# A graph network with a soft mixture of experts: the output product on 32-row strips

## The chip, the cores and the metric

The kernel runs on one core of a Trainium2 chip. The metric is the device time of one execution in microseconds (us); lower is better. The core has TensorE (PE in the profile; its weight loads are PEld), VectorE (DVE), ScalarE (ACT), GpSimd (POOL) and SyncE (SP), and 16 DMA engines.

## The reference

6250 nodes with 768 numbers each, 106250 edges sorted by destination. Two graph convolutions over the layer-normed input, added to it; then a soft mixture of experts with 8 experts of 4 slots each, 32 slots in all, added again:

```python
x = x + gnn(layernorm(x), edges, W1, b1, W2, b2)          # two GCN layers
# ffn on layernorm(x), m = 6250 tokens, n = 8 experts, p = 4 slots
logits  = einsum('bmd,dnp->bmnp', Xn, sp)
D = softmax(logits, axis=1)                                # over the tokens
C = softmax(logits over n*p, axis=2)                       # over the 32 slots of a token
X_tilde = einsum('bmd,bmnp->bnpd', Xn, D)                  # [32 slots, 768]
H = gelu(einsum('bnpd,ndh->bnph', X_tilde, W_down) + b_down)
Y_tilde = einsum('bnph,nhd->bnpd', H, W_up) + b_up         # [32 slots, 768]
Y = einsum('bnpd,bmnp->bmd', Y_tilde, C)                   # the output product
x = x + Y
```

## The kernel before

Nodes lie in T = 49 tiles of 128 (the last has 106). Each engine has its own program; semaphores order them. All arithmetic is in f32 but for the one-hot products of the start.

**Start.** SP loads the edges' destinations; VectorE makes one-hot matrices of them in 25 groups (L897 and L899, both operands in SBUF), and TensorE counts with them (L1274). GpSimd clears and fills the constants one after the other: iotas, memsets, two selects on `own_expert` and two on `in_quarter` (the loops at L604 and L608), then selects that make `ident`, `below` and `steps_down` (L615 to L620), each of which counts up `ready_consts`. TensorE begins behind all three. Behind `steps_down` GpSimd's queue issues the first weight loads (L627). TensorE turns each weight, and ScalarE moves it away (L698) between groups of statistics over x (L713, L724); it then scales x and stores it as the first layer's table. `in_quarter` is a [128, 4] table of masks: column c is 1 on the rows 32c to 32c + 31 and 0 elsewhere.

**Layers.** Both layers gather neighbours' rows with indirect DMAs (L659), sum them on VectorE (L1113) and multiply by the weights on TensorE.

**Experts.** TensorE mixes all tokens into the 32 slots (L1430), applies the down weights (L1447), and, after the gelu, the up weights (L1455, and the bias with 8 rows at L1457). The left operand holds each slot four times, so that `acc` gets Y_tilde four times, one copy on each strip of 32 rows.

**Output product.** The coefficients `cw` of four tiles at a time (a group; there are 13, the last holds tile 48 alone) are turned by one transpose (`turn_c`, L1465) into `work`, and ScalarE copies them to one of two `cT` buffers (L872): rows 32c to 32c + 31 of it belong to tile 4g + c. To take the right rows, VectorE makes four masked copies of `acc` (L1248, into hid, the two self_row buffers and agg; tile t uses copy t mod 4, `y_quarters`), each zero outside of its own strip. Tile t's product then contracts all 128 rows of `cT` with copy t mod 4, in two halves of 384 columns; each half shows up as two records, so a tile has four (L1479). It writes to one of three pairs of PSUM banks in turn (acc, fixed, left), and starts only when the add of tile t - 3 has read its pair. VectorE adds the tile to x in an output buffer (L1255). ScalarE's queue issues the store (L865), and tile t's store waits until that of tile t - 4 has landed. The copy of the next group's cT stands in the same queue ahead of a group's stores. The last 16 tiles of x do not fit and are loaded again by SP (L500): five before this stage, eleven in it, each behind an early tile's store.

Of the kernel before, what the change touches and what calls it, by code (L numbers as in the profile page):

```python
# [11 lines left out]
P = 128  # L12
# [4 lines left out]
H = D // 2  # L17
# [14 lines left out]
EXPERTS, SLOTS_PER, HID = 8, 4, D // 8  # L32
SLOTS = EXPERTS * SLOTS_PER
# [23 lines left out]
def build(nc, a):  # L57
# [6 lines left out]
    ALU = mybir.AluOpType  # L64
# [3 lines left out]
    with ctx:  # L68
        def sb(name, shape, dt=f32):
            return ctx.enter_context(nc.sbuf_tensor(name, shape, dt))  # L70
# [4 lines left out]
        def sem(name):  # L75
            return ctx.enter_context(nc.semaphore(name))
# [49 lines left out]
        self_row = sb("self_row", [P, 2, D])  # L126
        agg = sb("agg", [P, D])
# [3 lines left out]
        hid = sb("hid", [P, D])  # L131
# [3 lines left out]
        bup = sb("bup", [EXPERTS, D])  # L135
        sel = sb("sel", [EXPERTS, 4, SLOTS])
        own_expert = sb("own_expert", [SLOTS, EXPERTS])
        in_quarter = sb("in_quarter", [P, 4])
        hidT = sb("hidT", [HID, SLOTS])
        hid_blocks = sb("hid_blocks", [HID, EXPERTS * BLOCK])  # L140
        cT = sb("cT", [P, 2, P])
# [4 lines left out]
        acc = ps("acc", [P, 2, 512])  # L146
# [7 lines left out]
        def halves(ap):  # L154
            return ap.rearrange("p (h n) -> p h n", h=2)
# [55 lines left out]
        def layer_sems(l):  # L211
# [10 lines left out]
        F = {n: sem("F_" + n) for n in (  # L222
            "turned", "w_in", "w_staged", "mixed_done", "out_ready", "c_turned", "c_moved", "y_done", "blocks_clear",
            "exp_in", "exp_done", "root_in", "root_done", "gelu_in", "gelu_done", "top_ready", "sumd_ready", "sumd_done",
            "c_ready", "mix_ready", "mixT_ready", "down_done", "down_picked", "up_done", "y_slots_ready")}
# [153 lines left out]
        def full(i, k, t):  # L379
# [24 lines left out]
        accs = [acc, fixed, left]  # L404
        hid_lhs = hid_blocks[:, 0:EXPERTS * P].rearrange("p (n c) -> p n c", n=EXPERTS)
        hid_own = hid_blocks[:, :].rearrange("p (n c) -> p n c", c=BLOCK)[:, :, 0:P].rearrange(
            "p n (c q) -> p n c q", c=4)[:, :, :, 0:SLOTS_PER]
        y_quarters = [hid[:, :], self_row[:, 0, :], self_row[:, 1, :], agg[:, :]]
        ffn = flat[:, 4 * D + T * SLOTS:]
        wdown = WT[0][:, :, :].rearrange("p k (n h) -> p k n h", n=EXPERTS)  # L410
        wup = ffn[0:HID, 0:EXPERTS * D].rearrange("p (n d) -> p n d", n=EXPERTS)
# [178 lines left out]
        def _(pool):  # L590
# [7 lines left out]
                pool.memset(ap, v).then_inc(s["cleared"], 1)  # L598
            pool.memset(hid_blocks[:, :], 0.0).then_inc(F["blocks_clear"], 1)
            pool.memset(own_expert[:, :], 1.0).then_inc(F["blocks_clear"], 1)  # L600
            pool.memset(in_quarter[:, :], 1.0).then_inc(F["blocks_clear"], 1)
            pool.wait_ge(F["blocks_clear"], 3)
            for ap, width, cols in ((own_expert[:, :], SLOTS_PER, EXPERTS), (in_quarter[:, :], SLOTS, 4)):
                pool.affine_select(out=ap, in_=ap, compare_op=ALU.is_ge, fill=0.0, base=0, pattern=[[-width, cols]],  # L604
                                   channel_multiplier=1).then_inc(F["blocks_clear"], 1)
            pool.wait_ge(F["blocks_clear"], 5)
            for ap, width, cols in ((own_expert[:, :], SLOTS_PER, EXPERTS), (in_quarter[:, :], SLOTS, 4)):
                pool.affine_select(out=ap, in_=ap, compare_op=ALU.is_gt, fill=0.0, base=width, pattern=[[width, cols]],  # L608
                                   channel_multiplier=-1).then_inc(F["blocks_clear"], 1)
            pool.iota(zero_row[:, :], pattern=[[1, 1]], base=ZERO_ROW, channel_multiplier=1,  # L610
                      allow_small_or_imprecise_dtypes=True).then_inc(s["iotas"], 1)
            pool.iota(slot_of[:, :], pattern=[[P, PICKS]], base=0, channel_multiplier=1,
# [3 lines left out]
                               base=0, pattern=[[-1, P]], channel_multiplier=1).then_inc(s["ready_consts"], 1)  # L616
            pool.affine_select(out=below[:, :], in_=ones[:, :], compare_op=ALU.is_gt, fill=0.0,
                               base=0, pattern=[[1, P]], channel_multiplier=-1).then_inc(s["ready_consts"], 1)
            pool.wait_ge(s["ready_consts"], 1)
            pool.affine_select(out=steps_down[:, :], in_=ident[:, :], compare_op=ALU.not_equal, fill=-1.0,  # L620
                               base=-1, pattern=[[-1, P]], channel_multiplier=1).then_inc(s["ready_consts"], 1)
# [63 lines left out]
        def _(act):  # L685
# [54 lines left out]
            for n in range(RELOADED, len(loads)):  # L740
                t = loads[n]
# [111 lines left out]
                    act.wait_ge(F["exp_in"], len(THIRDS) + 1)  # L853
                    act.activation(cw[:, :, :], cw[:, :, :], ACT.Exp).then_inc(F["exp_done"], 1)
            act.wait_ge(F["gelu_in"], 1)
            act.wait_ge(F["blocks_clear"], 7)
            act.activation(hid_own, hidT[:, :].rearrange("p (n q) -> p n q", n=EXPERTS).unsqueeze(2)
                           .to_broadcast([HID, EXPERTS, 4, SLOTS_PER]), ACT.Gelu).then_inc(F["gelu_done"], 1)

# [22 lines left out]
        def _(dve):  # L882
# [345 lines left out]
                                     ident[0:EXPERTS, 0:EXPERTS].unsqueeze(1).unsqueeze(3)  # L1228
                                     .to_broadcast([EXPERTS, 4, EXPERTS, SLOTS_PER])))
            dve.wait_ge(F["down_done"], 1)  # L1230
            dve.wait_ge(F["blocks_clear"], 7)
            spread = hid[0:SLOTS, :].rearrange("p (n h) -> p n h", n=EXPERTS)
            for h in range(2):
                ns = slice(h * EXPERTS // 2, (h + 1) * EXPERTS // 2)
# [9 lines left out]
                                       bdT.unsqueeze(2).to_broadcast([HID, EXPERTS, SLOTS_PER]), ALU.add))  # L1244
            dve.sem_inc(F["gelu_in"], 1)
            dve.wait_ge(F["up_done"], 1)
            for c, y in enumerate(y_quarters):
                dve.tensor_scalar(halves(y), acc[:, :, 0:H], in_quarter[:, c:c + 1], None, ALU.mult  # L1248
                                  ).then_inc(F["y_slots_ready"], 1)
            for t in range(T):  # L1250
                dve.wait_ge(F["y_done"], t + 1)
                if t >= KEPT:
# [6 lines left out]
        def _(pe):  # L1259
# [205 lines left out]
                pe.transpose(tp[0:cols, g % 2, 0:P], cw[:, 4 * g:4 * g + cols // SLOTS, :].rearrange("p t q -> p (t q)"),  # L1465
                             ident[:, :]).then_inc(F["c_turned"], 1)
            turn_c(0)
            pe.wait_ge(F["y_slots_ready"], 4)
            for g in range(QUADS):
                if g + 1 < QUADS:  # L1470
                    turn_c(g + 1)
                pe.wait_ge(F["c_moved"], g + 1)
                ts = range(4 * g, min(4 * g + 4, T))
                for t in ts:
                    if t >= 3:
                        pe.wait_ge(F["out_ready"], t - 2)
                    k = SLOTS * len(ts)
                    for h in range(2):
                        m = pe.matmul(accs[t % 3][:, h, 0:H], cT[0:k, g % 2, :], y_quarters[t % 4][0:k, h * H:(h + 1) * H],  # L1479
                                      start=True, stop=True)  # L1480
                    m.then_inc(F["y_done"], 1)

# [22 lines left out]
```

## Time and profile before

| | us |
|---|---|
| median of 3 runs | 3048.95 (3045.4 to 3049.35) |
| span of the profiled execution, first to last instruction | 2757.7 |
| TensorE busy | 2105.0 (76%) |
| VectorE busy | 1809.1 (66%) |
| GpSimd busy | 1840.6 (67%) |
| ScalarE busy | 535.4 (19%) |

The profiled execution is given by its span alone; the time that it took in all stands nowhere in the page. The median of the runs is 291.25 us above the span, which holds what lies ahead of the first instruction and behind the last. The mean granted TensorE clock is 0.934 of full speed.

### The profile page before, as it was taken

How to read it: one execution, taken by the hardware profiler on the slowest of the kernel's cores; microseconds unless marked ns; L12 is line 12 of the kernel's file. 1: busy time of each engine (PE TensorE's matmuls, PEld its weight loads, DVE VectorE, ACT ScalarE, POOL GpSimd, SP SyncE). 2: the span in 40 equal slices, each digit the busy share in tenths (PEclk: the TensorE clock that was granted, in tenths of full speed). 3: DMA queues.
4: the chain of work that ended last, by engine and by line, in shares of the span. 5: the costliest groups of instructions: out<-in, count | busy, mean ns of one | idle time of the engine just before them, and what ended most of it. 6: DMA issues, size and time to landing. Idle time of an engine off the chain costs nothing.

```text
span 2757.7 us, 27634 instructions
## 1 busy us (share of the span) xinstructions
PE 2105.0 (76%) x7712; PEld 1248.5 (45%) x7713; DVE 1809.1 (66%) x2350; ACT 535.4 (19%) x985; POOL 1840.6 (67%) x1853
## 2 busy tenths in 40 slices
PE   6716777777787777787768877787787787888888
PEld 6703444444444444444434544444444454545334
DVE  7755666666676667666556766676766666666226
ACT  7950111111111111111101212211121222221310
POOL 3157777777777777777567777777777777776000
PEclk9999999999989989989978999999999999899899
DMA  9498999999999999999779999999999999998738
GB/s 331 155 411 304 315 321 322 322 321 322 322 325 327 327 329 326 325 317 319 269 278 328 373 341 339 338 339 342 344 346 344 342 342 343 336 338 306 252 111 322
DMA packets 237825, 876.71 MB, mean 318 GB/s; under 512 B 63260, under 2 KB 64044, under 8 KB 237756
## 3 DMA queue, kind: packets, MB, share of 16 engines
q0 software_dynamic: 143808, 671.74, 69.2%
q1 hardware_dynamic: 66132, 162.17, 16.0%
q10 hardware_dynamic: 27836, 42.21, 4.2%
q8 instruction: 23, 0.38, 0.1%
q14 instruction: 26, 0.21, 0.0%
HBM read 826.10 MB, written 82.00 MB: 329 GB/s over the span
## 4 chain that ended last, share of the span: by engine, by line
DMA 31%; POOL 26%; issue 16%; PE 12%; DVE 9%; ACT 4%; POOLq 0%; DVEq 0%; ACTq 0%
DMA rows<-table_layer,gidx 28%; POOL rows L659 26%; DVE acc L1113 6%; PE work L1355 3%; PE left L1381 3%; PE left L1430 2%; DMA table_layer<-xstage 2%; DVE agg L1113 1%; ACT logits L724 1%; ACT xsT L713 1%; DVE agg L1158 1%; DMA out_x<-xstage 1%; PE acc L1479 1%; ACT acc L783 1%; PE work L1367 1%
## 5 line engine op out<-in xcount | busy, mean ns | idle before, releaser
L659 POOL DMA_INDIRECT rows<-table_layer,gidx x1764 | 1761.6, 999 | 537.9 <-issue 449.4
L1113 DVE TENSOR_TENSOR acc<-acc,rows 128x768 f32<-128x768 f32 x1176 | 1134.7, 965 | 705.7 <-DMA rows<-table_layer,gidx 651.6
L1381 PE MATMUL left<-rows,hot 128*128 128x384 f32 x1960 | 847.9, 561 | 455.5 <-DMA rows<-table_layer,gidx 448.3
L1355 PE MATMUL work<-WT,aggT 128*128 128x384 f32 x2352 | 798.7, 497 | 43.9 <-DVE row_idx L1022 42.5
L1381 PEld LDWEIGHTS left<-rows,hot 128*128 128x128 f32 x1960 | 369.4, 209 | 792.8 <-DMA rows<-table_layer,gidx 625.7
L1355 PEld LDWEIGHTS work<-WT,aggT 128*128 128x128 f32 x2352 | 453.8, 195 | 386.8 <-DVE row_idx L1022 76.0
L783 ACT ACTIVATE acc<-rows 128x768 f32<-128x768 f32 x98 | 79.8, 814 | 667.1 <-DVE agg L1158 582.2
L813 ACT ACTIVATE aggT<-fixed 128x768 f32<-128x768 f32 x98 | 79.4, 810 | 514.1 <-PE fixed L1331 514.1
L800 ACT ACTIVATE xsT<-fixed 128x768 f32<-128x768 f32 x49 | 39.7, 810 | 459.1 <-PE fixed L1342 459.1
L793 ACT ACTIVATE ynext<-hid,dinv 128x768 f32<-128x768 f32 x49 | 45.8, 934 | 339.0 <-DVE hid L1128 339.0
L1158 DVE TENSOR_TENSOR agg<-left,agg 128x768 f32<-128x768 f32 x98 | 93.9, 958 | 8.7
L1113 DVE TENSOR_TENSOR agg<-acc,self_row 128x768 f32<-128x768 f32 x98 | 93.8, 958 | 4.4
L1274 PE MATMUL left<-rows 125*128 125x49 bf16 x850 | 79.2, 269 | 19.8 <-POOL steps_down L620 19.8
L1331 PEld LDWEIGHTS fixed<-ident,agg 128*128 128x128 f32 x588 | 71.8, 143 | 38.4 <-issue 17.6
L1331 PE MATMUL fixed<-ident,agg 128*128 128x128 f32 x588 | 82.3, 277 | 6.8 <-DVE agg L1158 6.8
L1274 PEld LDWEIGHTS left<-rows 125*128 125x128 bf16 x850 | 78.4, 142 | 20.1 <-POOL steps_down L620 19.5
L1367 PEld LDWEIGHTS work<-sp_c,xsT 128*128 128x128 f32 x588 | 75.5, 197 | 16.2 <-ACT xsT L800 3.0
L1072 DVE TENSOR_TENSOR hot<-acc,left_node 128x640 f32<-128x640 f32 x98 | 79.9, 815 | 0.4 <-DVE xsT L1049 0.4
L634 POOL DMA_INDIRECT rows<-src_windows,ynext x49 | 51.4, 1049 | 42.6 <-DVEq L937 28.0
L1367 PE MATMUL work<-sp_c,xsT 128*128 128x32 f32 x588 | 72.4, 275 | 3.2 <-ACT xsT L800 2.5
L1297 PEld LDWEIGHTS work<-xsT,before_end 128*128 128x128 f32 x490 | 65.9, 201 | 16.0 <-DVE before_end L994 2.4
L897 DVE TENSOR_TENSOR rows<-rows 125x4352 bf16<-125x4352 bf16 x25 | 60.6, 2424 | 17.6 <-PE left L1274 17.6
(307 smaller groups left out, 1253.2 us busy)
## 6 DMA issues: line engine op xcount, KB each, us to landing
self_row<-table_layer SPq DMA_DIRECT2D x98, 384.0 KB, 6.6
rows<-table_layer,gidx POOLq DMA_INDIRECT x1764, 5.7
xstage<-in_x SPq DMA_DIRECT2D x67, 384.0 KB, 8.1
xs<-in_x SPq DMA_DIRECT2D x58, 384.0 KB, 7.5
xnew<-xs SPq DMA_DIRECT2D x49, 384.0 KB, 5.0
table_layer<-ynext SPq DMA_DIRECT2D x48, 384.0 KB, 5.1
table_layer<-xstage ACTq DMA_DIRECT2D x40, 384.0 KB, 11.6
xstage<-xnew SPq DMA_DIRECT2D x21, 384.0 KB, 5.8
```

What stands on the lines that cost most here:

```text
L659: pool.indirect_dma_start(rows[:, slot, :], None, table[l][0:ROWS, :], bass.IndirectOffsetOnAxis(ap=gidx[:, k % 2, slot:slot + 1], axis=0) ...
L783: act.activation(acc[:, :, 0:H], halves(rows[:, SLOT["own", 0], :]), ACT.Copy).then_inc(S["first_copied"], 1)
L813: act.activation(halves(aggT[:, :, :].rearrange("p k n -> p (k n)")), turned[:, :, 0:H], ACT.Copy).then_inc(S["aggT_ready"], 1)
L1072: dve.tensor_tensor(hot[:, b, 0:LEFT, :], iota_ps.unsqueeze(1).to_broadcast([P, LEFT, P]), left_node[:, ds(t, 1), 0:LEFT].rearrange("p t c ...
L1113: dve.tensor_tensor(acc[:, :, 0:H] if n < OWN - 1 else halves(agg[:, :]), acc[:, :, 0:H], halves(row), ALU.add).then_inc(S["added"], 1)
L1158: dve.tensor_tensor(halves(agg[:, :]), left[:, :, 0:H], halves(agg[:, :]), ALU.add).then_inc(S["agg_ready"], 1)
L1274: m = pe.matmul(mm[:, 0, 0:T], oh_low[:, g % 2, :, j], oh_high[:, g % 2, :, j], start=(g == 0 and j == 0), stop=(g == GROUPS - 1 and j == ...
L1297: m = pe.matmul(found[:, c // 3, c % 3, :], before_end[:, c * P:(c + 1) * P], cands[:, ds(t, 1), :], start=True, stop=True)
L1331: m = pe.transpose(turned[:, kc // 3, (kc % 3) * P:(kc % 3 + 1) * P], agg[:, kc * P:(kc + 1) * P], ident[:, :])
L1355: m = pe.matmul(work[:, h, 0:H], aggT[:, kc, :], WT[l][:, kc, h * H:(h + 1) * H], start=kc == 0, stop=kc == KC - 1)
L1367: m = pe.matmul(work[:, 1, H:H + SLOTS], xsT[:, 0, kc, :], sp_c[:, kc, :], start=kc == 0, stop=kc == KC - 1)
L1381: m = pe.matmul(left[:, h, 0:H], hot[:, b, c, :], rows[:, slot, h * H:(h + 1) * H], start=c == 0, stop=c == LEFT - 1)
```

## The change

The masks, their memset and their two selects go; the semaphore `blocks_clear` ends at 4 instead of 7. One plain copy of `acc` into hid takes the place of the four masked ones. Tile t's product contracts only the 32 rows of its own strip, on both operands. The number of matmuls and their columns stay.

```diff
-        in_quarter = sb("in_quarter", [P, 4])
...
-        y_quarters = [hid[:, :], self_row[:, 0, :], self_row[:, 1, :], agg[:, :]]
+        y_copies = hid[:, :]
...
-            pool.memset(in_quarter[:, :], 1.0).then_inc(F["blocks_clear"], 1)
+            pool.wait_ge(F["blocks_clear"], 2)
+            pool.affine_select(out=own_expert[:, :], in_=own_expert[:, :], compare_op=ALU.is_ge, fill=0.0, base=0,
+                               pattern=[[-SLOTS_PER, EXPERTS]], channel_multiplier=1).then_inc(F["blocks_clear"], 1)
             pool.wait_ge(F["blocks_clear"], 3)
-            for ap, width, cols in ((own_expert[:, :], SLOTS_PER, EXPERTS), (in_quarter[:, :], SLOTS, 4)):
-                pool.affine_select(out=ap, in_=ap, compare_op=ALU.is_ge, fill=0.0, base=0, pattern=[[-width, cols]],
-                                   channel_multiplier=1).then_inc(F["blocks_clear"], 1)
-            pool.wait_ge(F["blocks_clear"], 5)
-            for ap, width, cols in ((own_expert[:, :], SLOTS_PER, EXPERTS), (in_quarter[:, :], SLOTS, 4)):
-                pool.affine_select(out=ap, in_=ap, compare_op=ALU.is_gt, fill=0.0, base=width, pattern=[[width, cols]],
-                                   channel_multiplier=-1).then_inc(F["blocks_clear"], 1)
+            pool.affine_select(out=own_expert[:, :], in_=own_expert[:, :], compare_op=ALU.is_gt, fill=0.0, base=SLOTS_PER,
+                               pattern=[[SLOTS_PER, EXPERTS]], channel_multiplier=-1).then_inc(F["blocks_clear"], 1)
...
             dve.wait_ge(F["up_done"], 1)
-            for c, y in enumerate(y_quarters):
-                dve.tensor_scalar(halves(y), acc[:, :, 0:H], in_quarter[:, c:c + 1], None, ALU.mult
-                                  ).then_inc(F["y_slots_ready"], 1)
+            dve.tensor_copy(halves(y_copies), acc[:, :, 0:H]).then_inc(F["y_slots_ready"], 1)
...
-            pe.wait_ge(F["y_slots_ready"], 4)
+            pe.wait_ge(F["y_slots_ready"], 1)
...
-                    k = SLOTS * len(ts)
+                    strip = slice(SLOTS * (t % 4), SLOTS * (t % 4 + 1))
                     for h in range(2):
-                        m = pe.matmul(accs[t % 3][:, h, 0:H], cT[0:k, g % 2, :], y_quarters[t % 4][0:k, h * H:(h + 1) * H],
+                        m = pe.matmul(accs[t % 3][:, h, 0:H], cT[strip, g % 2, :], y_copies[strip, h * H:(h + 1) * H],
                                       start=True, stop=True)
```

## Rows read from the trace of the kernel before

**Rows 1.** The page, chain that ended last, by line, share of the span

```profile
DMA rows<-table_layer,gidx 28%; POOL rows L659 26%; DVE acc L1113 6%; PE work L1355 3%; PE left L1381 3%; PE left L1430 2%; DMA table_layer<-xstage 2%; DVE agg L1113 1%; ACT logits L724 1%; ACT xsT L713 1%; DVE agg L1158 1%; DMA out_x<-xstage 1%; PE acc L1479 1%; ACT acc L783 1%; PE work L1367 1%
```

**Rows 2.** Windows over the output stage: length, busy us, PEclk, DMA share, GB/s

```profile
2688.00:2707.80 19.80, 19.13 (x62) 10.98 (x61) 14.48 (x16) 0.82 (x3) 0.00 (x0) 1.00 1.02 402
...
2714.30:2724.00 9.70, 9.63 (x31) 5.74 (x32) 5.93 (x7) 0.57 (x3) 0.00 (x0) 1.00 1.03 412
2724.00:2748.60 24.60, 23.64 (x76) 13.36 (x74) 17.98 (x19) 1.10 (x4) 0.00 (x0) 1.00 0.77 303
2748.70:2757.70 9.00, 0.00 (x0) 0.00 (x0) 0.00 (x0) 0.00 (x0) 0.00 (x0) 0.59 0.14 50
```

**Rows 3.** The chain in order of time: start us, us, what

```profile
2673.51 1.50 PE acc L1457 x4
...
2679.36 2.56 PE acc L1479 x4
...
2740.89 0.11 PE work L1465
...
2744.87 1.29 PE left L1479 x4
2746.16 1.50 PE acc L1479 x4
```

**Rows 4.** Timeline: start us, us, engine, line; idle before in brackets

```profile
2673.44 0.94 PEld L1457 LDWEIGHTS acc<-bup,sel 8*128 8x128 f32 x4 [0.55 <-issue]
...
2675.04 1.02 DVE L1248 TENSOR_SCALAR hid<-acc,in_quarter 128x768 f32<-128x768 f32 x1 [14.25 <-PE acc L1457]
...
2677.82 1.01 DVE L1248 TENSOR_SCALAR agg<-acc,in_quarter 128x768 f32<-128x768 f32 x1
...
2746.09 0.94 PEld L1479 LDWEIGHTS acc<-hid,cT 32*128 32x128 f32 x4 [0.55 <-issue]
```

**Rows 5.** Windows around the copies, columns as in rows 2

```profile
2675.30:2678.80 3.50, 0.00 (x0) 0.00 (x0) 3.50 (x4) 0.27 (x1) 0.00 (x0) 0.98 0.00 0
2678.80:2681.80 3.00, 2.92 (x6) 1.71 (x7) 0.03 (x1) 0.28 (x1) 0.00 (x0) 0.50 0.00 0
```

**Rows 6.** Timeline of the start

```profile
14.46 1.02 DVE L899 TENSOR_TENSOR rows<-rows 125x1666 bf16<-125x1666 bf16 x1
14.55 0.98 POOL L604 TENSOR_SCALAR_AFFINE_SELECT in_quarter<-in_quarter 128x4 f32<-128x4 f32 x1
...
15.39 2.42 DVE L897 TENSOR_TENSOR rows<-rows 125x4352 bf16<-125x4352 bf16 x1
15.60 2.26 POOL L608 TENSOR_SCALAR_AFFINE_SELECT own_expert<-own_expert 32x8 f32<-32x8 f32 x1
...
17.73 1.02 DVE L899 TENSOR_TENSOR rows<-rows 125x1666 bf16<-125x1666 bf16 x1
...
17.82 0.97 POOL L608 TENSOR_SCALAR_AFFINE_SELECT in_quarter<-in_quarter 128x4 f32<-128x4 f32 x1
...
18.96 0.28 POOL L615 TENSOR_SCALAR_AFFINE_SELECT ident<-ident 128x128 f32<-128x128 f32 x1
...
19.45 0.28 POOL L620 TENSOR_SCALAR_AFFINE_SELECT steps_down<-ident 128x128 f32<-128x128 f32 x1
...
27.81 0.82 ACT L698 ACTIVATE WT<-work 128x768 f32<-128x768 f32 x1 [3.38 <-PE work L1267]
```

**Rows 7.** Timeline: the plain copies from PSUM on VectorE

```profile
156.98 0.55 DVE L1049 COPY xsT<-left 128x377 f32<-128x377 f32 x1 [1.84 <-PE left L1305]
...
2647.46 0.36 DVE L1223 COPY aggT<-work 128x192 f32<-128x192 f32 x1 [0.73 <-PE work L1442]
```

**Rows 8.** Groups by line from 2660 us on: xcount, busy us, mean ns, idle before

```profile
L1255 DVE TENSOR_TENSOR xstage<-acc,xstage 128x768 f32<-128x768 f32 x7 | 6.7, 958 | 2.6 <-PE acc L1479 2.6
```

**Rows 9.** Windows over the mix of all tokens (L1430), columns as in rows 2

```profile
2600.00:2620.00 20.00, 20.00 (x63) 6.82 (x62) 0.27 (x1) 6.36 (x17) 0.00 (x0) 1.00 0.48 116
```

**Rows 10.** Waits of TensorE in the output stage: us in total, times, longest

```profile
PE acc L1479 <- ACT cT L872: 1.0, 1, 1.0
```

More of the change, by code:

```diff
@@ L855, in _ @@
             act.wait_ge(F["gelu_in"], 1)
-            act.wait_ge(F["blocks_clear"], 7)
+            act.wait_ge(F["blocks_clear"], 4)
             act.activation(hid_own, hidT[:, :].rearrange("p (n q) -> p n q", n=EXPERTS).unsqueeze(2)
@@ L1230, in _ @@
             dve.wait_ge(F["down_done"], 1)
-            dve.wait_ge(F["blocks_clear"], 7)
+            dve.wait_ge(F["blocks_clear"], 4)
             spread = hid[0:SLOTS, :].rearrange("p (n h) -> p n h", n=EXPERTS)
```

## The prediction

> **What bounds the kernel now.** I read the page first, for where the edited stages lie in the chain of waits. Gathers and their issue on GpSimd hold 28% and 26% of it, in layers that the diff does not touch; the output product, PE acc at L1479, shows up with 1% [rows 1]. So three short places count: the start of the program, the copies ahead of the output product, and the output stage, together under 100 of 2757.7 us.
>
> The output stage comes next, cut into stretches [rows 2]. From 2688 to 2724 the DMA engines are full, 402 to 412 GB/s: stores of finished tiles and reloads of the last sixteen share them. From 2724 to 2748.6 they move 303 GB/s and TensorE is busy 23.6 of 24.6 us. The last 9 us are the last store (50 GB/s), and they follow the last add whatever the stage before did. So the stage is bound by transfers first and by TensorE later. The chain in order of time gives the pace of the second part: 1.29 us for a tile's four matmul records, 0.11 us for the transpose between groups of four, 1.50 us for the last tile [rows 3]. A group of four tiles is 4 x 1.29 + 0.11 = 5.27 us.
>
> The timeline ahead of it shows the four masked copies one after the other, while TensorE does nothing [rows 4], and the windows give the granted clock: 0.98 in that gap, 0.50 just after it (the 1.2 GHz level) [rows 5], 1.00 again later [rows 2]. The last view is the first 28 us, where the removed GpSimd work sits [rows 6].
>
> **The start of the program.** Three GpSimd instructions go: a memset and two selects on in_quarter, 0.98 and 0.97 us by their durations [rows 6]. TensorE cannot start before steps_down, and GpSimd's first weight load is issued right behind it; ScalarE then waits 3.38 us for that weight's transposes and is busy from there without a gap. An earlier load therefore moves everything behind it. Adding up the rows gives about 2.0 us. But the rows say more: selects on 128x4 and 32x8 take 0.98, 2.26 and 0.97 us, while those on 128x128 take 0.28 each. The three slow ones end at 15.53, 17.86 and 18.79 us (start plus duration), each 0.04 or 0.05 us behind the end of a VectorE one-hot operation (15.48, 17.81, 18.75); the fast ones run once VectorE is idle. I take it that a select gets through once per VectorE operation. Then without in_quarter the select on ident comes through at 17.86, below at 18.79, and steps_down ends at about 19.05 instead of 19.73: 0.7 us gained, not 2.0. I take 0.7 and keep 2.0 for the range.
>
> That reading has a rule behind it. The Trainium skill ("SBUF — State Buffer", on the shared port pair) says that a GpSimd operation which reads SBUF and a VectorE operation with two SBUF inputs lock each other out for a whole instruction; the ends in these rows agree. By the rule the saving is 0.7 us, by the durations alone 2.0.
>
> **The copies.** Before, from the first copy's start to the end of tile 0 by the chain takes 2681.92 - 2675.04 = 6.88 us: 3.80 of copies, 0.52 with the transpose, 2.56 for four matmul records at half clock [rows 3, 4]. After, there is one plain copy. No row shows a plain copy of 128x768 from PSUM; two smaller ones take 0.36 us at 192 columns and 0.55 at 377 [rows 7], a slope that gives 0.95, and the masked one takes 1.02. I take 0.99. TensorE's gap, which by the chain begins at 2675.01, then ends at about 2676.07 instead of 2678.84. Since the clock was still 0.98 in the gap and fell only at its end, I count full clock afterwards: 0.25 for the transpose and 1.50 for the tile, the price of the only 32-row tile that the trace has. That is 0.99 + 0.04 + 0.25 + 1.50 = 2.78, a gain of 4.10 us. If the clock fell all the same, 1.4 of this is lost; that bound is kept. The stage that follows is bound by transfers, and since those start earlier by the same time and carry the same bytes, the 4.10 us pass through it.
>
> **The output products.** Each tile has four records before and after, with 384 columns; only the rows shrink, from 128 to 32. Fewer rows alone buy nothing: the last tile with 32 rows and the bias product with 8 (L1457) take no less than a full one. What changes is the neighbours. Two costs or gains come in.
>
> First, a switch between full-height and 32-row products. Both 8-row (L1457) and 32-row (last tile) groups take 1.50 us instead of 1.29, and in both the weight load is not pulled ahead but starts behind 0.55 us of idle [rows 3, 4]. So 0.21 us per entry; I give the same to the way back, which no row prices apart (at least nothing, at most the 0.55 us of that idle). Before, this is paid at the very end; after, each group holds one full-height transpose between strips, so 2 x 0.21 = 0.42 us per group.
>
> Second, neighbouring tiles now sit in different 32-row strips of the array and write to different PSUM tiles (acc, fixed, left). No row here has two products in different strips, so the price is bounded: at worst nothing overlaps (1.29 per tile), at best VectorE's add becomes the limit, 0.96 us per tile [rows 8], about 4.2 us per group with handovers. In between lies what an in-order engine could do: records of one tile share a strip and stay serial, so only the last record of a tile can run beside the first of the next, and four tiles take 16 - 3 = 13 slots of 0.3225 us, 4.19 us. I take this middle value because the switch cost shows that TensorE treats 32-row products as a mode of their own.
>
> The Trainium skill ("TensorE: Matmul & The Clock Gate", Part 3) states that matmuls in different row groups run concurrently while a single one with 32 rows costs as much as with 128; its "TensorEngine Tiling (Array Packing)" adds that changing the mode drains the engine. The second speaks against the change and agrees with the 0.21 us here; the first no row shows.
>
> Sum per group: 4.19 + 0.11 + 0.42 = 4.72, against 5.27: 0.55 us less. It counts only where TensorE is the limit, behind the stretch in which transfers rule. The last tile starts at 2746.16; counted back at 5.27 us, six full groups (tiles 24 to 47) fit from about 2714.5 on, which is where that stretch gives way: 6 x 0.55 = 3.3 us. In the groups before, extra or saved time hides behind the full DMA queue. The last tile no longer has a switch ahead of it and can overlap tile 47: 1.50 becomes 0.97, 0.5 us. Against this, the DMA engines are full until 2724, and ScalarE's queue holds each cT copy behind the stores of the group before, which wait for earlier stores to land. A faster TensorE meets that wait once more; I set 0.5 us for it, half of the 1.0 us that it idles for ahead of tile 24 now [rows 10].
>
> **The sum.** -0.7 - 4.1 - 3.3 - 0.5 + 0.5 = -8.1 us. Made against the profiled execution, whose span is 2757.7: 2749.6 after. Its time outside the span is not given; the median of the runs, 3048.95, lies 291.25 above the span, and nothing in the change touches that part. So 3048.95 - 8.1 = 3040.9 us. The runs shown spread from 3045.4 to 3049.35; about 0.2%, 6 us, is what a measurement tells from no change.
>
> **Rivals.**
> **No overlap between strips.** Switches cost and nothing is given back: 6 x 0.42 = 2.5 lost, 0.2 won at the last tile, so -0.7 - 4.1 + 2.3 = -2.5: 3046.5 us. For it: no overlapping products in the trace, and TensorE's f32 products go as two records each, of which I do not know whether they keep the array to themselves. Against it: only that 32-row groups are visibly handled apart. The result would be within 0.2%.
> **Free switches.** If the drain seen at the last tile hides behind other strips' work, a group is bound by the add: 4.2 + 0.1 us, six groups give 5.8 instead of 3.3, and 3038.4 us.
> **The clock falls in the output stage.** With a quarter of the rows in use, the granted clock might drop to the 1.2 GHz level for whole stretches. A tile then costs 2.56 us [rows 3]; at 13 slots of 0.64 a group takes about 8.7 us, twelve groups and a tile 107 us from 2676.3 to 2783, against 2747.7: some 35 us more, 3084 us. It decides from about eleven slow tiles in the second part on (11 x 1.27 = 14 us eat the 8.1 and 6 more). Against it: the stage before the experts keeps TensorE at 1.00 with products of only 32 columns of weights [rows 9], and the 8-row and 32-row groups ran at full pace, though for 1.5 us only.
> **The rest of the program answers.** The gathers hold the largest share of the chain, and their arrivals can shift with an earlier start: I allow the 4 us by which the runs shown differ, either way.
>
> **How the numbers follow.** Overlap as forecast, with the free-switch case as its upper end: 0.62. No overlap: 0.30. Clock: 0.04. Anything else: 0.04. The likeliest case reaches from 3036 to 3044; the range takes in no overlap with its spread, and below, free switches with the 2.0 us start (3037.1) and the spread of the runs: 3034 to 3048. Within the overlap case three of four chances lie beyond 0.2% faster, in the others hardly one in ten: faster 0.50, within 0.2% 0.44, slower 0.06.
>
> **What the profile after would show.** The first steps_down at about 19.05 us, ident's select lengthened to about 2 us; one VectorE copy of 1.0 us ahead of the product; granted clock 1.00 right behind it; tile 0 done 4 us earlier within the stage; starts of records of neighbouring tiles closer than 0.32 us at the edges between tiles, 4.7 us per group behind tile 24; 303 GB/s raised to about 335. A pace of 5.7 us per group shows the first rival, granted clock near 0.5 the third. I am wrong above all if strips do not overlap, or if the earlier transfers do not come through the full-queue stretch.

## The result, and the profile after

The median of nine runs after is 3064.82 us (3056.27 to 3071.34), beside 3048.95 (3038.65 to 3053.65) for nine runs of before: ratio 1.0053, 95% interval 1.0041 to 1.0064. The change costs 0.5%, 15.9 us; 8.1 us of gain were forecast.

Chips differ: on those of the experiments before takes 2759.0 to 2759.4 us instead of 3049, and the ratio is the same (1.0052). The profiled execution of before (span 2757.7) is of that faster kind. So spans are compared below within one kind of chip, or by stretches of the output stage, which hold no gathers.

The page of after, busy time by engine: TensorE has 111 us more than before (2105.0), in as many matmuls.

```profile
PE 2216.2 (72%) x7712; PEld 1319.0 (43%) x7713; DVE 1808.2 (59%) x2347; ACT 533.5 (17%) x985; POOL 1838.7 (60%) x1850
```

Not all of it is the change's: 91 us are products of the layers (L1349), which take 540 ns each on this chip, with 238.0 us of idle ahead of them in all, and 497 ns in the profile of before, with 43.9. On the other kind of chip the two kernels have 2113.2 and 2131.9 us, 18.7 apart. Where these are, the windows of the output stage show; after, columns as in rows 2 (length, busy us, PEclk, DMA share, GB/s):

```profile
2969.00:2971.00 2.00, 1.91 (x6) 0.80 (x5) 0.31 (x1) 0.06 (x1) 0.00 (x0) 1.00 0.00 0
2971.00:2975.00 4.00, 3.30 (x13) 1.42 (x13) 0.64 (x1) 0.50 (x2) 0.00 (x0) 0.51 0.00 0
...
2980.00:2990.00 10.00, 9.66 (x29) 4.32 (x25) 4.11 (x5) 0.55 (x2) 0.00 (x0) 0.50 0.98 334
2990.00:3000.00 10.00, 9.33 (x22) 4.25 (x21) 5.86 (x7) 0.28 (x1) 0.00 (x0) 0.50 1.03 377
...
3040.00:3050.00 10.00, 9.33 (x24) 4.06 (x21) 6.25 (x7) 0.28 (x1) 0.00 (x0) 0.50 0.49 190
```

The granted clock falls to 0.50 (1.2 GHz) as before [rows 5], but it never comes back: 0.50 to the end, where before had 1.00 [rows 2]. A closer window shows that it fell during the copy, ahead of the first strip, which starts at 2972.11:

```profile
2971.20:2972.10 0.90, 0.40 (x1) 0.18 (x1) 0.44 (x1) 0.02 (x1) 0.00 (x0) 0.50 0.00 0
```

So what has to be explained is not the fall, which before has too, but that the clock stays down. The DMA engines, full at first, end at half of their share. The timeline shows the strips at work (start us, us, engine, line; idle before in brackets):

```profile
2970.69 0.96 DVE L1243 COPY hid<-acc 128x768 f32<-128x768 f32 x1 [14.25 <-PE acc L1451]
...
2971.70 0.48 PE L1459 MATMUL work<-ident,rows 128*128 128x128 f32 x1 [0.79 <-DVE hid L1243]
...
2972.11 1.00 PE L1473 MATMUL acc<-hid,cT 32*128 32x384 f32 x1
...
2972.12 1.00 PE L1473 MATMUL fixed<-hid,cT 32*128 32x384 f32 x1
...
2972.13 1.00 PE L1473 MATMUL left<-hid,cT 32*128 32x384 f32 x1
```

Three tiles start 0.01 us apart and run beside each other in full, not at their edges only. In the later groups two start together and the third some 0.7 us behind, when its pair of banks comes free. The chain in order of time gives the cost of a group:

```profile
2975.07 0.97 DVE slot_iota L1249
2976.03 0.04 issue
2976.08 2.92 PE acc L1473 x4
2979.00 0.41 PE work L1459
2979.41 0.93 PE fixed L1473
...
2982.30 0.97 DVE xstage L1249
2983.27 0.04 issue
```

The fourth tile waits for a free pair of banks and runs alone, 2.92 us; then a transpose, 0.41; then the next three tiles together, 2.89 (2979.41 to 2982.30); then the add that frees a pair and its hand-over, 1.01. Together 7.23 us, beside 5.27 before. Twelve groups and the last tile: 88.2 us from the start of tile 0 to the last add, where before took 69.3; the part ahead of tile 0, from the up weights on, shrinks from 18.1 to 15.3. So +18.9 and -2.8 make +16.1, beside 15.9 measured.

In the table, *stretch* runs from the first product with the up weights to the end of the last add, and *tail* from there to the end of the span. Experiments ran beside before on chips of the faster kind (2759.0 to 2759.4 us).

| kernel | median us | ratio (95%) | stretch | tail |
|---|---|---|---|---|
| before | 3048.95 | | 87.4 | 9.1 |
| after | 3064.82 | 1.0053 (1.0041, 1.0064) | 103.5 | 9.2 |
| r0_before | 2759.56, one run | | 86.9 | 9.0 |
| r1_after | 2773.78 | 1.0052 (1.0039, 1.0066) | 103.2 | 9.3 |
| e1_full_height | 2754.93 | 0.9984 (0.9975, 0.9993) | 82.6 | 9.0 |
| e2_one_strip | 2822.63, one run | | 150.8 | 9.0 |
| e3_half_height | 2756.81 | 0.9992 (0.9982, 1.0001) | 85.6 | 9.6 |
| e4_strips_ahead | 2746.33 | 0.9963 (0.9950, 0.9977) | 66.0 | 21.0 |
| e5_full_ahead | 2750.39 | 0.9972 (0.9963, 0.9981) | 82.5 | 9.0 |
| e6_half_ahead | 2750.28 | 0.9970 (0.9957, 0.9982) | 63.0 | 25.5 |
| e7_three_ahead | 2753.39 | 0.9979 (0.9969, 0.9989) | 82.4 | 9.1 |
| e8_one_half | 2823.24, one run | | 152.6 | 9.0 |
| e9_extra_full | 2781.01, one run | | 109.7 | 9.0 |

### The profile page after: what moved, and what is told of

Read it like the earlier page. It is cut to its first block, busy times and chain, and to the rows that moved or that the text cites. A ratio compares the mean times of both kernels' runs of the same rounds, so it can differ in the third digit from the quotient of the medians.

```text
span 3069.6 us, 27628 instructions
## 1 busy us (share of the span) xinstructions
PE 2216.2 (72%) x7712; PEld 1319.0 (43%) x7713; DVE 1808.2 (59%) x2347; ACT 533.5 (17%) x985; POOL 1838.7 (60%) x1850
## 4 chain that ended last, share of the span: by engine, by line
issue 24%; DVE 19%; another core or an unknown queue 15%; PE 14%; POOL 14%; DMA 10%; ACT 3%; DVEq 1%; POOLq 0%; ACTq 0%
POOL rows L655 13%; DVE acc L1109 13%; DMA rows<-table_layer,gidx 10%; PE work L1349 4%; PE left L1375 3%; PE left L1424 2%; ACT logits L720 1%; ACT xsT L709 1%; DVE work L1128 1%; DVE agg L1109 1%; DVE hot L1068 1%; PE acc L1473 1%; PE fixed L1473 1%; PE left L1473 1%
## 5 line engine op out<-in xcount | busy, mean ns | idle before, releaser
L1349 PE MATMUL work<-WT,aggT 128*128 128x384 f32 x2352 | 889.9, 540 | 238.0 <-DVE row_idx L1018 127.2
L1375 PE MATMUL left<-rows,hot 128*128 128x384 f32 x1960 | 827.1, 555 | 221.2 <-DMA rows<-table_layer,gidx 123.2
L1349 PEld LDWEIGHTS work<-WT,aggT 128*128 128x128 f32 x2352 | 500.7, 215 | 636.0 <-issue 245.7
L1375 PEld LDWEIGHTS left<-rows,hot 128*128 128x128 f32 x1960 | 386.8, 213 | 511.2 <-issue 196.9
L1336 PE MATMUL fixed<-ident,xs 128*128 128x128 f32 x294 | 69.0, 402 | 189.9 <-issue 184.6
L1114 DVE COPY logits<-work 128x32 f32 (+1 forms) x49 | 9.4, 191 | 261.1 <-remote 253.6
L1336 PEld LDWEIGHTS fixed<-ident,xs 128*128 128x128 f32 x294 | 52.9, 210 | 225.5 <-issue 218.9
L999 DVE TENSOR_TENSOR pick_col<-slot_of,work 128x6 f32<-128x6 f32 x49 | 7.9, 160 | 227.1 <-remote 219.9
L1291 PE MATMUL work<-xsT,before_end 128*128 (+1 forms) x490 | 64.3, 273 | 22.7 <-issue 22.6
```

The lines of the kernel that those rows point to most:

```text
L1291: m = pe.matmul(found[:, c // 3, c % 3, :], before_end[:, c * P:(c + 1) * P], cands[:, ds(t, 1), :], start=True, stop=True)
L1336: m = pe.transpose(turned[:, kc // 3, (kc % 3) * P:(kc % 3 + 1) * P], xs[:, side, kc * P:(kc + 1) * P], ident[:, :])
L1349: m = pe.matmul(work[:, h, 0:H], aggT[:, kc, :], WT[l][:, kc, h * H:(h + 1) * H], start=kc == 0, stop=kc == KC - 1)
L1375: m = pe.matmul(left[:, h, 0:H], hot[:, b, c, :], rows[:, slot, h * H:(h + 1) * H], start=c == 0, stop=c == LEFT - 1)
```

## The experiments

**r0_before and r1_after**: both kernels as they are, on a chip of the faster kind.

> The kernel before, once more, for a profile that stands beside the later ones. Theory (the 16 us were lost in the output stage): from the start of the up-weight products to the end of the last add it takes 87.4 us as in the first profile, and the span comes out near 3047, since in the changed kernel span and time differ by 1.7 us only. Rival (the loss lies in the gathers, which the profile of before showed too fast to judge): span far from the changed kernel's by more than the stage explains.

> The changed kernel once more, on the same chip as the kernel before and the experiments. Theory (16 us are lost between the start of the up-weight products and the last add, nowhere else): that stretch takes 103.5 us here too, granted clock 0.50 in the output stage, time about 2775.5 us, ratio 1.006. Rival (part of the loss belongs to the other chip's slower gathers): a ratio further from 1.006 with the same stretch.

The span of r0_before came out at 2757.8, not near 3047: that expectation missed, since this chip is of the faster kind. Stretch 86.9 and 103.2: the loss of 16.3 us sits in the output stage here too, at clock 0.50 to the end. The first window's DMA engines are full, the second's no longer:

```profile
2680.00:2706.00 26.00, 24.99 (x64) 11.32 (x65) 12.95 (x15) 1.11 (x4) 0.00 (x0) 0.50 1.00 367
2724.00:2763.70 39.70, 37.12 (x92) 16.67 (x90) 20.55 (x23) 1.38 (x5) 0.00 (x0) 0.50 0.57 225
```

**e1_full_height**: after's copy and start, but full-height products.

```diff
-                    strip = slice(SLOTS * (t % 4), SLOTS * (t % 4 + 1))
+                    strip = slice(0, SLOTS * len(ts))
```

> The changed kernel with one plain copy, but every product contracts all 128 rows again (this sums the shares of four tiles, so the output differs from the reference). It holds all of the change but the strips. Theory (the strips cost the time, through the clock): granted clock 1.00 in the output stage, 5.27 us per group of four tiles, up-weight products to last add 83.3 us, ratio about 0.9985. Rival (copy, freed GpSimd work or other places cost it): ratio near 1.005.

Windows, and the chain around tile 0:

```profile
2680.00:2706.00 26.00, 25.71 (x83) 15.05 (x82) 18.57 (x20) 1.11 (x4) 0.00 (x0) 1.00 1.01 390
2706.00:2742.00 36.00, 34.03 (x109) 19.29 (x107) 25.26 (x27) 1.93 (x7) 0.00 (x0) 1.00 0.86 339
```

```profile
2673.22 0.97 DVE hid L1243
2674.19 0.04 issue
2674.24 0.33 PE work L1459
2674.57 1.29 PE acc L1473 x4
```

The copies' part comes out as worked out: 2.64 us from the copy to the end of tile 0 instead of 6.88, the clock at 1.00 behind it in this profile (in e5's it falls all the same, see there), the stretch 4.3 shorter and the median 4.5 lower. With only the rows of the product changed back, the 103.2 us fall to 82.6: the loss belongs to the strips.

**e2_one_strip**: all tiles on strip 0, so that nothing runs beside anything. The rival to "few rows in use" was that short products with pauses or overlap among them pull the clock down.

```diff
-                    strip = slice(SLOTS * (t % 4), SLOTS * (t % 4 + 1))
+                    strip = slice(0, SLOTS)
```

> The changed kernel with every tile on strip 0 (each tile of a group then takes the first tile's coefficients, so the output differs from the reference). Products of 32 rows, serial, with no idle between them. Theory (few rows keep the clock at 1.2 GHz): granted clock 0.50, 2.56 us per tile, about 11 us per group, up-weight products to last add about 150 us. Rival (the idle of TensorE between the overlapped products, or the overlap itself, keeps it low): clock 1.00, 1.29 us per tile, 5.7 us per group, about 86 us.

A window of 60 us, and the chain:

```profile
2690.00:2750.00 60.00, 60.00 (x95) 29.50 (x94) 21.07 (x22) 1.39 (x5) 0.00 (x0) 0.50 0.58 209
```

```profile
2680.41 2.56 PE fixed L1473 x4
2682.97 2.56 PE left L1473 x4
```

TensorE is busy 60.00 of 60 us, with the same columns as full-height products, and stays at 0.50. So neither pauses nor overlap hold it down. (It fell at 2678.3, within the first tile behind the copy; what this run shows is that one strip at a time does not bring it back.) The Trainium skill ("TensorE: Matmul & The Clock Gate", Part 1) has the clock follow how busy the engine has been; here it was busy without a break, and the clock did not follow.

**e3_half_height**: before's kernel with two masked copies and 64-row products; tiles 4g and 4g + 1 contract rows 0 to 63, the other two rows 64 to 127.

```diff
-            for c, y in enumerate(y_quarters):
-                dve.tensor_scalar(halves(y), acc[:, :, 0:H], in_quarter[:, c:c + 1], None, ALU.mult
+            for c in range(2):
+                dve.tensor_scalar(halves(y_quarters[c]), acc[:, :, 0:H], in_parity[:, c:c + 1], None, ALU.mult
...
-                    k = SLOTS * len(ts)
+                    rows_c = slice(64 * (c // 2), 64 * (c // 2) + 64) if len(ts) == 4 else slice(0, SLOTS)
...
```

> Two masked copies (strips 0 and 2; strips 1 and 3), and each tile contracts 64 rows: tiles 0 and 1 of a group on the upper half, 2 and 3 on the lower. Output as the reference. Theory (rows in use decide the clock): either it falls as with 32 rows, then two tiles at most overlap and a group takes 2 x 2.6 to 4 x 2.6 us, 6 to 10 us, slower than before; or half of the rows are enough, then clock 1.00 and at most 5.3 us per group, up-weight products to last add 80 to 85 us. Rival (overlap itself lowers the clock): 0.50 here too.

```profile
2700.00:2710.00 10.00, 8.69 (x25) 5.05 (x22) 4.07 (x5) 0.28 (x1) 0.00 (x0) 0.67 1.03 416
2710.00:2720.00 10.00, 10.00 (x23) 5.12 (x20) 5.03 (x6) 0.56 (x2) 0.00 (x0) 0.56 0.78 312
2720.00:2730.00 10.00, 10.00 (x39) 5.94 (x39) 8.36 (x10) 0.56 (x2) 0.00 (x0) 1.00 0.85 336
```

```profile
2729.26 1.48 PE acc L1482 x4
2730.74 0.32 PE fixed L1482
2731.06 0.11 PE left L1482
...
2732.14 1.29 PE acc L1482 x4
2733.43 0.26 PE work L1467
```

Both levels occur, which neither theory nor rival had expected. The clock fell twice, at 2698.3 and at 2705.1, each time within 1 us behind a pause of 1.3 us at full DMA engines; the second time it stayed at 0.50 until 2718.7, though TensorE was busy without a break from 2706 on. From there it held 1.00 to the last add. At full clock a group takes 4.43 us (2729.26 to 2733.69): two neighbours in different halves share 1.40 us (2730.74 to 2732.14), the two others run alone. That pace, faster than 5.27, is taken back by the 17 us at low clock within the stage, and the ratio is not told from no change. I read it as "64 rows of a product are enough". That reading fell with e8.

**e8_one_half**: e3 with all products in one half.

```diff
-                    rows_c = slice(64 * (c // 2), 64 * (c // 2) + 64) if len(ts) == 4 else slice(0, SLOTS)
+                    rows_c = slice(0, 64) if len(ts) == 4 else slice(0, SLOTS)
```

> As e3_half_height, but every tile uses the upper 64 rows, so that no two products can run at once (the lower half's coefficients are left out, so the output differs from the reference). Theory (the rows of a product decide the clock, 64 are enough with and without overlap): clock 1.00, 1.29 us per tile, up-weight products to last add 84 to 87 us. Rival (32 rows fail and 64 succeed only because two of them overlap): clock 0.50, 2.56 us per tile, about 150 us.

```profile
2690.00:2750.00 60.00, 60.00 (x94) 29.46 (x93) 21.06 (x22) 1.54 (x6) 0.00 (x0) 0.50 0.57 209
```

64-row products one behind the other stay at 0.50 like 32-row ones: the rival's 0.50 and about 150 us came in (152.6). In e3 the full clock came with two halves in use beside each other for a part of each group. What goes with the clock in e1, e2, e3, e6 and e8 is the rows in use at one time, not the rows of a product. Whether 64-row products alone would keep a clock that is already at 1.00, e8 doesn't tell: it had fallen at 2677.1, ahead of the first product, which starts at 2677.8.

**e4_strips_ahead**: after, with what keeps four strips from running together taken away. All 13 transposes are made behind the mix of all tokens, into acc and fixed; ScalarE moves them into self_row and cT while the experts' weights are at work; work becomes a fourth pair of banks.

```diff
-        accs = [acc, fixed, left]
+        accs = [acc, fixed, left, work]
...
-                    if t >= 3:
-                        pe.wait_ge(F["out_ready"], t - 2)
+                    if t >= 4:
+                        pe.wait_ge(F["out_ready"], t - 3)
...
-                        m = pe.matmul(accs[t % 3][:, h, 0:H], cT[strip, g % 2, :], y_copies[strip, h * H:(h + 1) * H],
+                        m = pe.matmul(accs[t % 4][:, h, 0:H], cg[strip, :], y_copies[strip, h * H:(h + 1) * H],
```

> The changed kernel with all thirteen transposes of the coefficients made behind the mix of the tokens, into two PSUM tensors and moved to SBUF in four copies, and with a fourth PSUM pair for the output products. Four strips can then run at once and no full-height product lies between them. Theory (the lost time is the half clock times one lone fourth tile per group): even at clock 0.50 four tiles take 2.6 to 2.9 us of TensorE, so VectorE's adds (0.9 us each) and the DMA engines rule, up-weight products to last add 74 to 79 us, ratio 0.996. If the clock depends on the rows in use, four strips at once bring it back to 1.00, and the time is the same. Rival (the overlapped products are slowed by something else): above 87 us, no gain over before.

```profile
2674.00:2675.00 1.00, 1.00 (x12) 0.40 (x4) 0.00 (x0) 0.00 (x0) 0.00 (x0) 0.50 0.00 0
2676.00:2679.00 3.00, 2.48 (x10) 1.66 (x11) 3.00 (x5) 0.00 (x0) 0.00 (x0) 1.00 0.57 212
2680.00:2685.00 5.00, 5.00 (x23) 4.41 (x23) 4.67 (x6) 0.00 (x0) 0.00 (x0) 0.50 0.95 331
2685.00:2695.00 10.00, 10.00 (x44) 8.81 (x43) 9.02 (x11) 0.00 (x0) 0.00 (x0) 0.50 1.03 411
...
2725.00:2735.00 10.00, 0.00 (x0) 0.00 (x0) 0.00 (x0) 0.00 (x0) 0.00 (x0) 0.50 1.02 400
```

Behind four tiles side by side the clock came up to 1.00, once, for 3.4 us (2675.9 to 2679.4). From there each tile starts when an add frees its pair, they run staggered, and the clock is 0.50 again, with TensorE busy throughout. Even so three or four strips at 0.50 nearly keep up with VectorE, and the DMA engines are the bound: the last add ends 66.0 us into the stretch, earlier than the 74 to 79 expected, and stores at 400 GB/s run on behind it, so the tail is 21.0 instead of 9. This is the kernel with the lowest median, ahead of before and after (0.9963 of before).

**e5_full_ahead** (e4 with full-height products) and **e7_three_ahead** (e4 with three pairs) split e4's gain.

```diff
-                    strip = slice(SLOTS * (t % 4), SLOTS * (t % 4 + 1))
+                    strip = slice(0, SLOTS * len(ts))
```

```diff
-        accs = [acc, fixed, left, work]
+        accs = [acc, fixed, left]
...
```

> As e4_strips_ahead, but each product contracts all 128 rows of the one plain copy (the shares of four tiles are summed, so the output differs from the reference). Shows what the early transposes and the fourth buffer are worth without strips. Both theories: clock 1.00, TensorE at 4 x 1.29 = 5.16 us per group rules, up-weight products to last add about 81 to 82 us, 1.3 us less than with one copy alone, ratio 0.998.

> As e4_strips_ahead (early transposes, strips of 32 rows), but with three PSUM pairs as in the changed kernel: tells what the early transposes do and what the fourth pair does. Clock 0.50 is expected by all. Theory (the full-height transpose between groups and the wait of the fourth tile both cost; without the transpose tiles follow one another as buffers come free): a pair is taken for 2.6 us of product and 1.1 us of add, so three tiles in 3.7 us, 4.9 us per group, up-weight products to last add about 77 us, between 66 us (e4) and 103 us (the changed kernel). Rival (the fourth pair alone makes the gain): near 100 us, 7 us per group.

e5's stretch, 82.5, is e1's, 82.6, but not under equal clocks. In e5's profile the clock is at 0.50 behind the copy, from 2675.8 to 2682.5:

```profile
2676.54 2.90 PE acc L1471 x4
2679.44 2.56 PE fixed L1471 x4
2682.00 1.64 PE left L1471 x4
2683.64 1.29 PE work L1471 x4
```

The first three tiles take 7.10 us there, where three at full clock take 3.87, so some 3 us that early transposes and a fourth pair may give are hidden by the clock. With full-height products they give at most that (an estimate). Full-height products follow the one copy in e1 and in e5; in e5's profile the clock falls there and comes back, in e1's it doesn't fall.

With strips the transposes' move gives 103.2 - 82.4 = 20.8 us of stretch, since no group pays for a tile alone and for a transpose between strips, and the fourth pair another 82.4 - 66.0 = 16.4. The 77 us expected of e7 were 5 too few. e7 runs three tiles per 3.98 us, where 3.7 were expected (one acc product of the chain at 2701.94, the next at 2705.92), still at 0.50:

```profile
2701.94 0.96 PE acc L1471 x2
...
2705.92 0.96 PE acc L1471 x2
```

```profile
2690.00:2700.00 10.00, 10.00 (x34) 7.21 (x33) 6.40 (x8) 0.00 (x0) 0.00 (x0) 0.50 1.03 414
```

**e6_half_ahead**: e4 with e3's two masked copies and 64-row products.

```diff
-        y_copies = hid[:, :]
+        y_quarters = [hid[:, :], agg[:, :]]
...
-                    strip = slice(SLOTS * (t % 4), SLOTS * (t % 4 + 1))
+                    rows_c = slice(64 * (c // 2), 64 * (c // 2) + 64) if len(ts) == 4 else slice(0, SLOTS)
```

> As e4_strips_ahead, but with two masked copies and 64 rows per tile (tiles 0 and 1 of a group above, 2 and 3 below). Output as the reference. With 64 rows the clock stood at 1.00 where TensorE had work without a pause. Theory: upper and lower half run beside each other, a group needs 2.6 us of TensorE at full clock, adds and DMA engines rule, one more masked copy costs 0.9 us: up-weight products to last add 75 to 80 us, ratio 0.997. Rival: pauses at the full DMA engines let the clock fall to 0.50 and it does not come back, a group takes 5.2 us and the stretch about 83 us.

```profile
2685.00:2695.00 10.00, 10.00 (x48) 6.78 (x47) 10.00 (x13) 0.00 (x0) 0.00 (x0) 1.00 1.02 375
...
```

Halves beside each other hold 1.00 from 2681.5 to the last add; the stretch, 63.0, is far below the 75 to 80 expected. VectorE's adds are the limit (busy 10.00 of 10), then the stores: the stretch is 3.0 shorter than e4's and the tail 4.5 longer. So the low clock costs e4 little that the stores don't take anyway; the two ratios are not told apart.

**e9_extra_full**: after, with a full-height product of two halves, overwritten, ahead of each group, to see whether full rows now and then hold the clock.

```diff
+                    if t % 4 == 0 and len(ts) == 4:
+                        for h in range(2):
+                            pe.matmul(accs[t % 3][:, h, 0:H], cT[:, g % 2, :], y_copies[:, h * H:(h + 1) * H],
+                                      start=True, stop=True)
```

> The changed kernel with one more full-height product per group of four, ahead of its first tile and overwritten by it (the output stays). It adds work of 1.29 us at full clock, 2.56 us at half. Theory (full-height work between the strips can hold the clock): granted clock well above 0.50, a group in 5 to 7 us, up-weight products to last add 80 to 100 us, below the changed kernel's 103 us although more is computed. Rival (the strips pull the clock down whatever stands beside them): 0.50 throughout, 9.8 us per group, about 134 us.

```profile
2690.00:2700.00 10.00, 8.96 (x30) 3.76 (x31) 3.64 (x4) 0.50 (x2) 0.00 (x0) 0.67 0.99 374
2720.00:2730.00 10.00, 8.68 (x28) 4.06 (x29) 6.27 (x8) 0.28 (x1) 0.00 (x0) 0.79 0.56 224
```

The clock goes up and down and is 0.71 on average over the stage, with nothing else changed than full rows in one of five products. The added work costs more than that gives back, 109.7 us: a miss for the time that was expected, a hit for the clock. The first group has strips at full clock: three together take 1.5 us (2677.03 to 2678.52), the fourth alone 1.55 and the transpose 0.26:

```profile
2679.56 1.55 PE acc L1477 x4
2681.11 0.26 PE work L1459
```

## Why the prediction was wrong, step by step

- **What bounds the stage**: TensorE in its second part, as said; with the clock at 0.50 it is the bound in the first part too, in which savings and losses were to hide behind full DMA engines. And the last 9 us don't follow the last add whatever the stage does: behind e4's and e6's shorter stages the stores ran on for 21.0 and 25.5 us.
- **The start**: the reading "once per VectorE operation" held: ident's select takes 2.36 us, as foreseen. steps_down ends at 19.34 instead of 19.05, 0.4 us earlier than before [rows 6]; two VectorE operations got longer (2.51 and 1.11 us instead of 2.42 and 1.02), for a reason that no run shows. The 0.7 us can't be seen to arrive: the weight load, issued at 19.30, landed after 7.12 us, and ScalarE began at 28.04, where before began at 27.81. Other profiles of the same two kernels have 27.82 (r1_after) and 29.04 (r0_before), so the landing moves by more than the term. That e1's median and its stretch fall by about the same, 4.5 and 4.3 us, leaves little for it.

```profile
15.71 2.36 POOL L611 TENSOR_SCALAR_AFFINE_SELECT ident<-ident 128x128 f32<-128x128 f32 x1
18.03 1.07 POOL L613 TENSOR_SCALAR_AFFINE_SELECT below<-ones 128x128 f32<-128x128 f32 x1
19.06 0.28 POOL L616 TENSOR_SCALAR_AFFINE_SELECT steps_down<-ident 128x128 f32<-128x128 f32 x1
...
28.04 0.82 ACT L694 ACTIVATE WT<-work 128x768 f32<-128x768 f32 x1 [3.48 <-PE work L1261]
```

- **The copies**: a plain copy takes 0.96 (0.99 taken). The 4.10 us came in e1 (4.2 to the end of tile 0), but in after only 2.5 of them: 4.34 us from the copy's start to the end of the first three tiles, since the transpose and the tiles behind it ran at half clock. "Since the clock was still 0.98 in the gap and fell only at its end, I count full clock afterwards" was a wrong step, with any rows behind it: in after the clock fell at 2971.1, before the first strip; in e5, with full-height products, it fell behind the one copy too; in e1's profile it didn't. The bound that was kept for it, 1.4 us, is about what it cost.
- **The output products, the step that failed**: the 4.19 us of tiles per group were worked out with 0.3225 us per record, the full clock's, against a rival of 0.04 in which the clock falls. It fell, and stayed down for the whole stage. The two rows set against that rival could not carry it: products of 32 columns use all 128 rows and say nothing of rows [rows 9]; and 1.50 us for the 8-row and the last 32-row group were too short to see the clock answer [rows 3]. The row that should have weighed was that before's clock was at 0.50 at tile 0 and had to come back by work of some kind [rows 5]; strips are other work. In place of the 4.72 us forecast for a group, 7.23 were measured, in each of the twelve full groups and not only behind tile 24.
- **Overlap**: more of it than the 13 slots. Three strips run side by side, the third of them one record behind in the later groups, and the fourth tile runs alone. That is why the clock rival's own price, 35 us, was too high: a group took 7.23, not 8.7. Neither "no overlap" nor the edges-only case was right. It agrees with the Trainium skill ("TensorE: Matmul & The Clock Gate", Part 3), which has products in different row groups run concurrently: starts 0.01 us apart here.
- **Switches**: at full clock, in e3 with its 64-row products, the transpose costs 0.26 us in the chain instead of 0.11, and the tile behind it 1.48 instead of 1.29: 0.34 for the two switches, where 0.42 was taken. That term was of about the right size, and it was not what decided.
- **The 291.25 us "above the span"** were no work outside the span. Each execution's time lies 1.7 or 1.8 us above its own span (3071.34 and 3069.6; 2759.56 and 2757.8); span and median came from chips of different kinds. It did no harm to the difference.

**What stays open.** The clock came back or held with halves beside each other, with full-height products, and once behind four strips started together; it stayed at 0.50 with one strip, with one half, with three strips (also started together), and with four staggered. That the strips keep the clock down is shown by e1, e2 and e9; that it is by the rows in use at a time is the reading that fits, not a thing shown. It does not fit e4: why its staggered strips stay at 0.50 where e6's halves hold 1.00, though the rows in use at a time look similar, no run tells. (Over a time the two differ: e6 has 184 records of 64 rows in 43 us from 2682 on, 4.3 per us, and e4 156 records of 32 rows in 38 us, 4.1 per us. No run separates rows side by side from rows put through.) Nor did strips ever run at full clock for long, so a group's pace there is an estimate from e9's first group: 1.5 for three tiles, 1.01 for the add and hand-over, 1.55 for the lone tile and 0.26 for the transpose, 4.3 us.

## What to carry to other kernels

A product on fewer rows costs TensorE the same time per record, and can cost it half of its clock: before cutting the contraction, ask what keeps many rows in use at a time, and read the granted clock of the stage first in the profile after. A gain by strips needs enough PSUM banks, and no full-height transposes among them, so that the strips run together; here that was worth 37 us of the stretch, of which some 27 arrived in the time (2773.78 to 2746.33), and turned the loss into a gain. The plain copy in place of four masked ones was worth its 4 us in e1, whose products sum the shares of four tiles; with strips the loss outweighs it.

## What the runs showed of the hardware that was not expected

- The granted clock stays at 0.50 through 60.00 us of unbroken TensorE work when only 32 rows, or only 64 rows, are in use at a time (e2, e8), and at 1.00 with two 64-row halves beside each other (e6) or with 128 rows (e1).
- Behind one and the same copy the clock fell in e5's profile, for 6.7 us, and not in e1's, with full-height products in both.
- Products on three or four 32-row strips start 0.01 to 0.05 us apart, each with full length, 0.64 us from record to record at half clock.
- Chips differ by some 290 us in this kernel: of the 296 us between after and r1_after up to the up weights, 274 lie between the first gather and the last (2598.0 and 2323.6 us). In the output stage they differ by less than 1 us (103.5 and 103.2 us of stretch).
